# A window-attention block on one core: the projection as one fp32 product, the output product on another engine, y1 kept by row halves, new instruction orders

## The chip, the cores and the metric

One of the eight cores of a Trainium2 chip runs the whole program. The metric is the device time of one execution in microseconds, given as the median of three runs. Everything is fp32 in and out.

## The reference

The input x is (4, 96, 128, 128): four images, 96 channels. The first layer is a shifted-window transformer block, the second a divisive normalisation:

```python
y = _ln(x, norm1_w, norm1_b)                       # over the 96 channels
y = roll(y, (-4, -4)); windows of 8 x 8 = 64 tokens
qkv = y @ qkv_w.T + qkv_b                          # 6 heads of 16
attn = softmax(q * 16**-0.5 @ k.T + mask)          # mask in the last row/column of windows
out = (attn @ v) @ proj_w.T + proj_b
x = shortcut + roll_back(out)
h1 = gelu(_ln(x, norm2_w, norm2_b) @ mlp_w1.T + mlp_b1)     # 96 -> 384
x = x + (h1 @ mlp_w2.T + mlp_b2)                   # 384 -> 96
out = x * rsqrt(beta_eff + gamma_eff @ (x * x))    # over the channels
```

## The kernel before

**Tiles.** A unit is one row of 16 windows of one image (1024 tokens), 64 units in all. The work goes by halves of a unit: 8 windows, 512 tokens, 128 halves. Most tiles are 96 channels (partitions) by 512 tokens.

**Rounds.** The program is software-pipelined. `rounds` (L221) unrolls rounds H = -5 to 127, and in each round every engine runs its list `steps` in a fixed, written-out order. A stage has an offset, so in round H the stage works on half H + offset: TURN_IN 4 (transpose x, statistics), TURN_OUT 3 (transpose the normalised values back, y1), QK 1 (keys and queries), ATTEND 0 (scores, softmax, values), PROJECT -1 (division, projection, first residual), MLP -2, SETTLE -3 (second MLP product, second residual, squares), DIVIDE -4 (denominators, outputs). Each engine works its list in order and waits on semaphores; nothing is reordered at run time. The last halves are finished by `late` calls behind the rounds.

**Products.** Large products are done in parts: `in_parts` (L949) splits weight and moving operand into a rounded part (hi) and a rest (lo) of type fp32r and adds three products, hi x hi, lo(weight) x hi and hi x lo. The splits of moving operands are made by GpSimd (`split_hi` L444, `split_lo` L449: y1, attended, squares, hidden) and VectorE. The attended values are split before the projection: VectorE divides (`divide`, L821) and rounds them (`round_attended`, L831), GpSimd subtracts (`rest_of_attended`, L462), TensorE projects in three parts (`project`, L1074). Small products, the transposes and the last projection (`last_project`, L1104) are one full fp32 product each.

**Tiles of TensorE.** Scores use tiles of 32 rows x 64 columns (L1013, masks L1021), values (L986), the sums of probabilities (L1066, L1069) and attend (L1056) write 32 columns at a time, the transposes of the first two probability groups (L1033) use 64 rows, all else the whole array.

**Banks.** The products of `MM_ITEMS` (L248) take turns in two PSUM banks, in the order of that list. A product waits until the product two places ahead has been read out of its bank (`mm_wait`).

**y1.** The first layer norm's result is held per unit as [window, token]. ScalarE writes it (`y_copy`, L555) four rows of each window at a time: an even half of a unit's transposes has the upper four rows of all 16 windows, the odd half the lower four. GpSimd's `round_y1` and `rest_of_y1` take these rows through `ln_rows` (runs of 32 values), and the products read a half of 8 windows as one contiguous run of 512.

**Output.** `outputs` (L850) on VectorE multiplies x3 by the inverse denominator into `o_ext`, 4 columns to the right; GpSimd copies the columns that wrap around the edge (`wrap_out`), and the SP queue stores the unit. SP also loads x and copies the keys into block form (`copy_keys`, 6 DMAs a half).

## Time and profile before

| | |
|---|---|
| median of 3 runs | 1819.56 us (1818.24 to 1821.19) |
| profiled execution | 1816.74 us, span in the trace 1814.5 us |
| mean granted TensorE clock | 0.995 of full |
| busy DVE / ACT / POOL | 1677.5 / 1587.7 / 1553.4 us |
| DMA | 81.17 MB, mean 45 GB/s |

PE is TensorE (PEld its weight loads, which run beside the products), DVE VectorE, ACT ScalarE, POOL GpSimd, SP the queue of DMAs. The trace's products overlap in a pipeline: the duration of one is longer than the distance to the next, so the distance between two starts is what a product takes of TensorE's time. One full fp32 product is recorded as two instructions, a transpose or an fp32r product as one.

### The profile page before, as it was taken

To read this page: it belongs to the slowest core of one execution; us is meant where nothing else is said; L and a number is where in the kernel's file an instruction comes from. 1 tells how busy PE (TensorE), PEld (TensorE's weight loads), DVE (VectorE), ACT (ScalarE), POOL (GpSimd) and SP (SyncE) were. 2 spreads that over 40 slices of the span, in tenths; PEclk is the share of its full clock that TensorE was granted. 3 is DMA by queue.
4 is the path that set the end of the run, shared out by engine and by line. 5 is a ranking of instruction groups with operands and counts; after the bars stand their busy time and mean duration, and the time that the engine had idled before them with its cause. 6 is when DMAs were issued, how large, how long until landed. Compare 5 with 4: busy or idle time off the path is not lost.

```text
span 1814.5 us, 78584 instructions
## 1 busy us (share of the span) xinstructions
PE 1764.4 (97%) x31203; PEld 1344.6 (74%) x31203; DVE 1677.5 (92%) x4637; ACT 1587.7 (87%) x2700; POOL 1553.4 (86%) x1661
## 2 busy tenths in 40 slices
PE   5899999999999999999999999999999999999997
PEld 3677777777777777777777777777777777777774
DVE  5799999999999999999999999999999999999985
ACT  2799999998999899989899999899989989998895
POOL 4488999988898888998898898898888889898883
PEclk9899999999999999999999999999999999999999
DMA  2111222122122122222121221221221221221211
GB/s 57 24 42 39 49 52 42 44 52 44 43 52 45 42 52 42 45 51 43 44 50 36 52 51 37 51 51 36 52 51 35 53 50 34 54 50 33 46 34 27
DMA packets 215143, 81.17 MB, mean 45 GB/s; under 512 B 116118, under 2 KB 214780, under 8 KB 214780
## 3 DMA queue, kind: packets, MB, share of 16 engines
q1 hardware_dynamic: 214218, 76.04, 19.2%
q8 instruction: 249, 4.08, 0.9%
q14 instruction: 114, 0.93, 0.2%
q10 hardware_dynamic: 562, 0.11, 0.0%
HBM read 25.75 MB, written 25.17 MB: 28 GB/s over the span
## 4 chain that ended last, share of the span: by engine, by line
PE 95%; DVE 1%; issue 1%; ACT 1%; DMA 0%; SPq 0%; POOL 0%; POOLq 0%; DVEq 0%; ACTq 0%
PE mm_bank L952 50%; PE score_banks L1013 7%; PE turn_bank L945 7%; PE turn_bank L938 6%; PE mm_bank L986 6%; PE pv_bank L1056 5%; PE score_banks L1033 5%; PE score_banks L1042 3%; PE mm_bank L1069 3%; PE mm_bank L1066 2%; PE score_banks L1021 1%; SPq L373 0%; PE mm_bank L1116 0%; DMA k_block<-k 0%; DMA x_ext<-in_x 0%
## 5 line engine op out<-in xcount | busy, mean ns | idle before, releaser
L452 POOL TENSOR_TENSOR hidden_lo<-hidden,hidden_hi 128x512 fp32r<-128x512 f32 x378 | 480.9, 1285 | 0.0
L539 ACT ACT_TABLE_LOAD x253 | 324.6, 1283 | 4.5
L452 POOL TENSOR_TENSOR attended_lo<-attended,attended_hi 96x512 fp32r<-96x512 f32 x127 | 163.8, 1290 | 111.0 <-DVE attended_hi L834 111.0
L808 DVE TENSOR_REDUCE row_max<-score_banks 128x8 f32<-128x512 f32 x384 | 241.4, 684 | 17.8 <-PE score_banks L1021 9.9
L582 ACT ACTIVATE probs<-shifted 128x512 f32<-128x512 f32 x384 | 236.4, 629 | 20.1 <-DVE shifted L816 13.2
L816 DVE TENSOR_TENSOR shifted<-score_banks,row_max 128x512 f32<-128x512 f32 x384 | 250.8, 680 | 0.0
L615 ACT ACTIVATE hidden<-mm_bank 128x512 f32<-128x512 f32 x381 | 228.6, 600 | 20.5 <-PE mm_bank L952 2.2
L447 POOL TENSOR_SCALAR hidden_hi<-hidden 128x512 fp32r<-128x512 f32 x378 | 228.5, 615 | 4.0 <-ACT hidden L615 3.8
L765 DVE BATCH_NORM_STATS2 stats<-turn_bank 128x6 f32<-128x96 f32 x1024 | 192.8, 250 | 30.2 <-PE turn_bank L938 25.8
L594 ACT ACTIVATE probs_t<-score_banks 128x512 f32<-128x512 f32 x384 | 214.5, 594 | 5.8 <-PE score_banks L1033 4.0
L468 POOL TENSOR_TENSOR x_sq<-x 96x512 f32<-96x512 f32 x126 | 130.7, 1037 | 73.7 <-DVE x L846 66.2
L945 PE MATMUL turn_bank<-ident_sb,y_tok 128*96 128x128 f32 x1024 | 161.1, 280 | 15.3 <-DVE y_tok L783 15.2
L952 PE MATMUL mm_bank<-y_hi,w_hi 97*128 97x512 f32 x381 | 171.8, 451 | 0.2 <-ACT hidden L615 0.2
L452 POOL TENSOR_TENSOR y_lo<-y,y_hi 96x512 fp32r<-96x512 f32 x128 | 163.4, 1276 | 1.1 <-POOL y_hi L447 1.1
L452 POOL TENSOR_TENSOR x_sq_lo<-x_sq,x_sq_hi 96x512 fp32r<-96x512 f32 x126 | 163.3, 1296 | 0.7 <-POOL x_sq_hi L447 0.7
L447 POOL TENSOR_SCALAR y_hi<-y 96x512 fp32r<-96x512 f32 x128 | 142.8, 1115 | 23.5 <-ACT y L564 23.5
L1013 PEld LDWEIGHTS score_banks<-k_block,q 32*64 32x64 f32 x6144 | 116.0, 132 | 51.9 <-issue 51.9
L1013 PE MATMUL score_banks<-k_block,q 32*64 32x128 f32 x6144 | 148.9, 275 | 4.7 <-DMA k_block<-k 3.6
L774 DVE TENSOR_TENSOR turn_bank<-turn_bank,moments 128x384 f32<-128x384 f32 x256 | 145.0, 566 | 9.0
L952 PE MATMUL mm_bank<-hidden_hi,w_hi 128*96 128x512 f32 x378 | 150.7, 399 | 0.9 <-ACT k L574 0.9
L952 PE MATMUL mm_bank<-y_lo,w_hi 97*128 97x512 f32 x381 | 150.9, 396 | 0.0
L952 PE MATMUL mm_bank<-y_hi,w_lo 97*128 97x512 f32 x381 | 150.3, 394 | 0.0
(144 smaller groups left out, 4815.3 us busy)
## 6 DMA issues: line engine op xcount, KB each, us to landing
x_ext<-in_x SPq DMA_DIRECT2D x128, 192.0 KB, 3.1
k_block<-k SPq DMA_DIRECT2D x768, 32.0 KB
out<-o_ext SPq DMA_DIRECT2D x128, 192.0 KB, 2.7
w_raw<-in_w_t SPq DMA_DIRECT2D x1, 144.0 KB
w<-in_w_t SPq DMA_DIRECT2D x1, 144.0 KB
qkv_raw<-in_qkv_t ACTq DMA_DIRECT2D x1, 108.0 KB
ident_sb<-in_ident SPq DMA_DIRECT2D x1, 64.0 KB, 2.3
q_quadrants<-in_qmask SPq DMA_DIRECT2D x3, 1.0 KB
```

What stands on the lines that cost most here:

```text
L447: nc.gpsimd.tensor_scalar(hi, whole, 1.0, 1.0, ALU.mult, ALU.mult).then_inc(hi_ready, 1)
L452: nc.gpsimd.tensor_tensor(lo, whole, hi, ALU.subtract).then_inc(is_split, 1)
L539: nc.scalar.preload_act_table_set(name)
L582: nc.scalar.activation(probs[:, g, :, :, :].rearrange("t p j k -> t (p j k)"), shifted[:, g, :, :].rearrange("t i k -> t (i k)"), ACT.Exp)\
L594: nc.scalar.activation(dst, src, ACT.Copy).then_inc(probs_t_ready, 1)
L615: nc.scalar.activation(hidden_of(A)[:, n, :], up_bank(A, n), ACT.Gelu).then_inc(gelu_ready, 1)
L765: made = nc.vector.bn_stats(stats[ln][:, c, :], turn_banks[ln][:, n * DIM:(n + 1) * DIM])
L808: nc.vector.tensor_reduce(row_max[:, g, :], group_scores(g), op=ALU.max, axis=AX.X)\
L816: nc.vector.tensor_tensor(shifted[:, g, :, :], group_scores(g), row_max[:, g, :].unsqueeze(2) .broadcast_to([128, PAIRS * TILE_HEADS, TOKE ...
L945: made = nc.tensor.transpose(turn_banks[ln][0:DIM, n * 128:(n + 1) * 128], y_tok[ln][:, c, :], ident_sb[:, :])
L952: made = nc.tensor.matmul(out, w, x_part, start=first and part == 0, stop=last and part == 2)
L1013: made = nc.tensor.matmul(score_banks[64 * n:64 * n + 64, r, cols], q[rows, unit_slot(a), (w + n) * TOKENS:(w + n + 1) * TOKENS], k_block[ ...
```

## The change

- `project` multiplies the whole (unsplit) fp32 tiles `wproj` and `attended` in one full fp32 product. The hi and lo tiles, `round_attended`, `rest_of_attended`, the weight split and `last_project` go; `divide` now waits until the projection of the half before has read `attended`.
- `outputs` moves from VectorE to GpSimd, behind `wrap_x` in its list; the last four halves' outputs stay on VectorE (`last_outputs`).
- y1, y1_hi and y1_lo are kept by row halves: [half of the rows, window, 32 tokens]. What `round_y1`, `rest_of_y1` and `y_copy` handle is one contiguous run of 512; the key and query products read it as 8 windows x 2 runs of 32, the value product's weights stay runs of 32.
- New orders on TensorE, VectorE, ScalarE and GpSimd, and in `MM_ITEMS`. On TensorE the value stage goes between the sums and the attend products, the denominators ahead of both transposes back, these ahead of the queries; the first up product ahead of the residual's transposes and the last probability group.

```diff
+            ("v", ATTEND, v_ready, 1, 1),
             ("k", QK, k_ready, 1, 1),
+            ("den", DIVIDE, log_den_made, 1, 1),
             ("q", QK, q_ready, 1, 1),
-            ("den", DIVIDE, log_den_made, 1, 1),
             ("mlp2", SETTLE, x3_ready, 1, 1),
-            ("v", ATTEND, v_ready, 1, 1),
...
+        def y1_rows(tile, a):
+            return half_of(tile[:, unit_slot(a), :], a)
+
+        def y1_windows(tile, a):
+            by_window = tile[:, unit_slot(a), :].rearrange("c (h n t) -> c n h t", h=2, t=TOKENS // 2)
+            return by_window[:, half_windows(a), :, :]
...
 GpSimd
+            def outputs(A, a):
+                wait_alone(pool, inv_den_ready, A + 1)
+                if has(A - 4):
+                    wait_alone(pool, out_stored[unit_slot(a)], 32 * (A // 4))
+                nc.gpsimd.tensor_tensor(windows_of(o_ext[:, unit_slot(a), :, :], a),
+                                        in_windows(half_of(x3, a)), in_windows(inv_den[:, :]),
+                                        ALU.mult).then_inc(out_ready, 1)
...
                 run(wrap_out, DIVIDE - 1)
-                run(rest_of_attended, PROJECT)
                 run(wrap_x, TURN_IN)
+                run(outputs, DIVIDE)
+                run(round_y1, TURN_OUT)
+                run(rest_of_y1, TURN_OUT)
                 run(square, SETTLE)
                 run(round_squares, SETTLE)
-                run(round_y1, TURN_OUT)
                 run(rest_of_squares, SETTLE)
-                run(rest_of_y1, TURN_OUT)
 ScalarE
                 run(k_copy, QK)
+                run(log_denominators, DIVIDE)
+                run(softmax_exp, ATTEND, 0)
+                run(inverse_denominators, DIVIDE)
+                run(softmax_exp, ATTEND, 1)
                 run(q_copy, QK)
                 run(y_copy, MLP, 1)
-                run(softmax_exp, ATTEND, 0)
-                run(log_denominators, DIVIDE)
-                run(inverse_denominators, DIVIDE)
-                run(softmax_exp, ATTEND, 1)
+                run(y_copy, TURN_OUT, 0)
                 run(softmax_exp, ATTEND, 2)
-                run(y_copy, TURN_OUT, 0)
                 run(load_tables, MLP, "gelu_and_others")
                 run(probs_t_copy, ATTEND, 0)
+                run(gelu, MLP, 0)
                 run(probs_t_copy, ATTEND, 1)
-                run(gelu, MLP, 0)
                 run(probs_t_copy, ATTEND, 2)
 VectorE
                 run(max_scores, ATTEND, 0)
                 run(max_scores, ATTEND, 1)
-                run(max_scores, ATTEND, 2)
+                run(v_blocks, ATTEND)
+                run(normalise, TURN_OUT, 0)
                 run(normalise, MLP, 1)
                 run(shift_scores, ATTEND, 0)
+                run(shift_scores, ATTEND, 1)
                 run(divide, PROJECT)
-                run(normalise, TURN_OUT, 0)
-                run(round_attended, PROJECT)
-                run(shift_scores, ATTEND, 1)
+                run(max_scores, ATTEND, 2)
                 run(shift_scores, ATTEND, 2)
                 run(second_residual, SETTLE)
                 run(split_y2, MLP)
-                run(v_blocks, ATTEND)
                 run(first_residual, PROJECT)
-                run(outputs, DIVIDE)
 TensorE
-                pe.wait_ge(attended_split, A + 1)
+                pe.wait_ge(attended_ready, A + 1)
                 mm_wait("proj", A)
-                in_parts(mm_bank("proj", A)[0:DIM, :], wproj_hi[:, :], wproj_lo[:, :],
-                         attended_hi[:, :], attended_lo[:, :]).then_inc(proj_made, 1)
+                nc.tensor.matmul(mm_bank("proj", A)[0:DIM, :], wproj[:, :], attended[:, :],
+                                 start=True, stop=True).then_inc(proj_made, 1)
...
                 run(scores, ATTEND)
                 run(sum_probs, ATTEND - 1)
+                run(project_v, ATTEND)
                 run(times_v, ATTEND - 1)
                 run(project_k, QK)
+                run(denominators, DIVIDE)
+                run(turn_out, TURN_OUT, 0)
+                run(turn_out, MLP, 1)
                 run(project_q, QK)
-                run(turn_out, MLP, 1)
-                run(denominators, DIVIDE)
                 for n in range(HID_CHUNKS):
                     run(mlp_down, SETTLE, n)
-                run(project_v, ATTEND)
-                run(turn_out, TURN_OUT, 0)
                 run(project, PROJECT)
                 run(turn_two_groups, ATTEND)
                 run(turn_in, TURN_IN, 0)
...
+                run(mlp_up, MLP, 0)
+                run(turn_in, PROJECT, 1)
                 run(turn_last_group, ATTEND)
-                run(mlp_up, MLP, 0)
                 run(mlp_up, MLP, 1)
-                run(turn_in, PROJECT, 1)
                 run(mlp_up, MLP, 2)
```

## Rows read from the trace of the kernel before

**Rows 1.** The page's busy times, shares of the span and numbers of instructions.
```profile
PE 1764.4 (97%) x31203; PEld 1344.6 (74%) x31203; DVE 1677.5 (92%) x4637; ACT 1587.7 (87%) x2700; POOL 1553.4 (86%) x1661
```
**Rows 2.** The chain that ended last, shares by engine.
```profile
PE 95%; DVE 1%; issue 1%; ACT 1%; DMA 0%; SPq 0%; POOL 0%; POOLq 0%; DVEq 0%; ACTq 0%
```
**Rows 3.** TensorE's waits from 100 to 1750 us: total, times, longest.
```profile
PE pv_bank L1056 <- issue: 5.5, 9, 0.8
...
```
**Rows 4.** Busy time (and instructions) by engine in a window, then clock and DMA.
```profile
900.00:927.00 27.00, 27.00 (x484) 20.71 (x483) 25.11 (x71) 24.50 (x43) 23.98 (x26) 1.00 0.21 47
```
**Rows 5.** Timeline of TensorE's products, one round: start, duration, instruction.
```profile
907.98 1.11 PE L1013 MATMUL score_banks<-k_block,q 32*64 32x128 f32 x48
...
911.73 0.40 PE L952 MATMUL mm_bank<-y_lo,wq_hi 97*96 97x512 f32 x1
911.96 0.60 PE L945 MATMUL turn_bank<-ident_sb,y_tok 128*96 128x128 f32 x4
912.32 0.47 PE L952 MATMUL mm_bank<-x_sq_hi,wgdn_hi 97*96 97x512 f32 x1
...
914.96 0.40 PE L952 MATMUL mm_bank<-hidden_lo,w_hi 128*96 128x512 f32 x1
915.28 0.89 PE L986 MATMUL mm_bank<-wv,y 97*32 97x48 f32 x64
916.10 0.64 PE L945 MATMUL turn_bank<-ident_sb,y_tok 128*96 128x128 f32 x4
916.50 0.47 PE L952 MATMUL mm_bank<-attended_hi,wproj_hi 97*96 97x512 f32 x1
...
917.37 0.71 PE L1033 MATMUL score_banks<-ident_sb,probs 64*128 64x64 f32 x16
...
921.39 1.12 PE L1013 MATMUL score_banks<-k_block,q 32*64 32x128 f32 x48
```
**Rows 6.** Timeline of weight loads of the last full fp32 products.
```profile
1800.54 0.16 PEld L1116 LDWEIGHTS mm_bank<-hidden,w 128*96 128x96 f32 x1 [0.27 <-issue]
...
1801.82 0.16 PEld L1116 LDWEIGHTS mm_bank<-hidden,w 128*96 128x96 f32 x1 [0.27 <-issue]
```
**Rows 7.** Timeline, products at the same place.
```profile
1799.87 0.39 PE L952 MATMUL score_banks<-y_lo,w_hi 97*128 97x512 f32 x1
1800.10 2.74 PE L1116 MATMUL mm_bank<-hidden,w 128*96 128x512 f32 x6
```
**Rows 8.** Timeline of weight loads in the sampled round, behind idle time.
```profile
909.02 0.12 PEld L1066 LDWEIGHTS mm_bank<-probs_t,ones_pair_sb 128*32 128x32 f32 x3 [0.17 <-issue]
...
915.28 0.75 PEld L986 LDWEIGHTS mm_bank<-wv,y 97*32 97x32 f32 x64 [0.40 <-issue]
```
**Rows 9.** GpSimd's groups; the first row gives least, middle and greatest ns.
```profile
L447 POOL TENSOR_SCALAR y_hi<-y x128: 612/1145/1156, 14.1 to 1738.3; 96x512 fp32r<-96x512 f32 x128
...
L452 POOL TENSOR_TENSOR attended_lo<-attended,attended_hi 96x512 fp32r<-96x512 f32 x127 | 163.8, 1290 | 111.0 <-DVE attended_hi L834 111.0
...
L468 POOL TENSOR_TENSOR x_sq<-x 96x512 f32<-96x512 f32 x126 | 130.7, 1037 | 73.7 <-DVE x L846 66.2 <-issue 7.3
...
L441 POOL COPY x_ext<-x_ext 96x32 f32<-96x32 f32 x64 | 13.3, 208 | 2.0 <-DMA x_ext<-in_x 1.7 <-POOL x_sq L433 0.3
```
**Rows 10.** VectorE's only squaring of x3 into x3_sq, as a group.
```profile
L756 DVE TENSOR_TENSOR x_sq<-x 96x512 f32<-96x512 f32 x1 | 0.7, 690 | 0.3 <-DVE x L846 0.3
```
**Rows 11.** Timelines of VectorE and GpSimd at 904.7 us.
```profile
904.72 0.68 DVE L853 TENSOR_TENSOR o_ext<-x,inv_den 96x512 f32<-96x512 f32 x1
...
904.73 1.14 POOL L447 TENSOR_SCALAR y_hi<-y 96x512 fp32r<-96x512 f32 x1
```
**Rows 12.** Timeline of ScalarE in the sampled round.
```profile
913.65 0.59 ACT L620 ACTIVATE log_den<-mm_bank 96x512 f32<-96x512 f32 x1
...
916.78 0.59 ACT L564 ACTIVATE y<-turn_bank 96x512 f32<-96x512 f32 x1 [0.48 <-PE turn_bank L945]
...
920.29 0.59 ACT L594 ACTIVATE probs_t<-score_banks 128x512 f32<-128x512 f32 x1
```

More of the change, by code:

```diff
@@ L57 @@
 MLP_CONSTS = 9
-MLP_WEIGHTS = 4
+MLP_WEIGHTS = 3
 TURN_IN, TURN_OUT, QK, ATTEND, PROJECT, MLP, SETTLE, DIVIDE = 4, 3, 1, 0, -1, -2, -3, -4
@@ L95, in window_block @@
         w2 = sb("w2", [128, HID_CHUNKS, DIM])
-        wq_hi, wq_lo, wk_hi, wk_lo, wproj_hi, wproj_lo, wgdn_hi, wgdn_lo = (
+        wq_hi, wq_lo, wk_hi, wk_lo, wgdn_hi, wgdn_lo = (
             sb(f"{name}_{part}", [DIM + 1, DIM], f32r)
-            for name in ("wq", "wk", "wproj", "wgdn") for part in ("hi", "lo"))
+            for name in ("wq", "wk", "wgdn") for part in ("hi", "lo"))
         w1_hi, w1_lo = (sb(f"w1_{part}", [DIM + 1, HIDDEN], f32r) for part in ("hi", "lo"))
@@ L427, in set_rows @@
             def set_rows():
-                for hi, lo in ((y2_hi, y2_lo), (attended_hi, attended_lo), (x3_sq_hi, x3_sq_lo)):
+                for hi, lo in ((y2_hi, y2_lo), (x3_sq_hi, x3_sq_lo)):
                     nc.gpsimd.memset(hi[DIM:DIM + 1, :].bitcast(f32), 1.0).then_inc(rows_set, 1)
@@ L454, in round_y1 @@
             def round_y1(A, a):
-                split_hi(ln_rows(y1_hi[0:DIM, unit_slot(a), :], a), ln_rows(y1[0:DIM, unit_slot(a), :], a),
+                split_hi(y1_rows(y1_hi, a)[0:DIM], y1_rows(y1, a)[0:DIM],
                          y_ready[0], y1_hi_ready, A + 1)
             def rest_of_y1(A, a):
-                hi, lo, whole = (ln_rows(tile[0:DIM, unit_slot(a), :], a) for tile in (y1_hi, y1_lo, y1))
+                hi, lo, whole = (y1_rows(tile, a)[0:DIM] for tile in (y1_hi, y1_lo, y1))
                 split_lo(hi, lo, whole, y1_hi_ready, y1_split, A + 1)
-            def rest_of_attended(A, a):
-                split_lo(attended_hi[0:DIM, :], attended_lo[0:DIM, :], attended[0:DIM, :],
-                         attended_hi_ready, attended_split, A + 1)
             def square(A, a):
@@ L823, in divide @@
                 dve.wait_ge(pv_made, A + 1)
+                wait(dve, proj_made, A)
                 for m in range(HEAD_PAIRS):
@@ L889, in _ @@
             late(statistics, FINAL, 1)
-            late(outputs, FINAL - 3)
+            last_outputs(FINAL - 3)
             late(normalise, FINAL, 1)
@@ L894, in _ @@
             late(last_squares, FINAL - 1)
-            late(outputs, FINAL - 2)
+            last_outputs(FINAL - 2)
             late(second_residual, FINAL)
             late(last_squares, FINAL)
-            late(outputs, FINAL - 1)
-            late(outputs, FINAL)
+            last_outputs(FINAL - 1)
+            last_outputs(FINAL)
         @block.tensor
@@ L962, in project_k @@
                 mm_wait("k", A)
-                rows = slice(0, DIM + 1)
                 in_parts(mm_bank("k", A)[0:DIM, :], wk_hi[:, :], wk_lo[:, :],
-                         half_of(y1_hi[rows, unit_slot(a), :], a), half_of(y1_lo[rows, unit_slot(a), :], a))\
+                         y1_windows(y1_hi, a), y1_windows(y1_lo, a))\
                     .then_inc(k_made, 1)
@@ L984, in project_v @@
                         for part in range(2):
-                            first, to = n * TOKENS + 32 * part, 64 * e + 32 * part
+                            to = 64 * e + 32 * part
                             made = nc.tensor.matmul(mm_bank("v", A)[to:to + 32, n * width:(n + 1) * width],
-                                                    half_of(y1[:, unit_slot(a), :], a)
-                                                    [:, first:first + 32],
+                                                    y1_windows(y1, a)[:, n, part, :],
                                                     wv[:, e, :, :], start=True, stop=True)
@@ L1102, in mlp_down @@
                     made.then_inc(mlp2_made, 1)
-            def last_project():
-                pe.wait_ge(attended_ready, FINAL + 1)
-                mm_wait("proj", FINAL)
-                nc.tensor.matmul(mm_bank("proj", FINAL)[0:DIM, :], wproj[:, :], attended[:, :],
-                                 start=True, stop=True).then_inc(proj_made, 1)
             def last_mlp_down(A):
@@ L1163, in _ @@
             late(denominators, FINAL - 3)
-            last_project()
+            late(project, FINAL)
             for n in range(HID_CHUNKS):
```

28 lines of the change are left out of this document (9 added, 19 removed).

## The prediction

> **What bounds the kernel now.** I read the shares of busy time first, then the chain, then who waited, then one round in order of time. TensorE is busy 1764.4 of 1814.5 us [rows 1], and the chain of work that ended last lies on it for 95% [rows 2]. From 100 to 1750 us its waits on all other engines and DMAs come to nothing: the list holds only stops "issue", 5.5 us in 9 pieces [rows 3]. In a sample of two rounds it is busy 27.00 of 27.00 us at full clock, VectorE 25.11, ScalarE 24.50, GpSimd 23.98 [rows 4]. So a round is as long as TensorE's own queue: from one score stage to the next 921.39 - 907.98 = 13.41 us [rows 5] (odd halves add mask products, which the change leaves alone). What the others do counts only if one of them, or a wait, becomes longer than TensorE's queue. The sum is therefore one of TensorE start-to-start intervals, not of busy times, which overlap.
>
> **Part 1, projection in full fp32.** Before: three fp32r products, from the first start at 916.50 to the start of the next stage at 917.37, 0.87 us [rows 5]. That holds 3 x 0.23 (an fp32r product that another follows without a switch takes 911.96 - 911.73 = 0.23), 0.09 for leaving the whole array for the small tiles of the probability transposes (the same step is 915.28 - 914.96 = 0.32 ahead of the value stage), and the remaining 0.09 for entering fp32r from another kind [rows 5]. After: one fp32 product, which the trace records as two instructions. At the end of the kernel such instructions load weights every (1801.82 - 1800.54)/3 = 0.427 us [rows 6], so the product takes 0.85 us, not less than the three that it replaces (0.70). Going over from fp32r to it costs nothing (1800.10 - 1799.87 = 0.23 [rows 7]), so the entry goes. The exit to small tiles no row shows behind an fp32 product: it is 0 at best and 0.09 as behind fp32r. I take 0.09, the nearest row. New stage 0.94 us: +0.07 a half; with a free exit -0.02.
>
> **Part 2, TensorE's order.** The value stage (32-column tiles) moves from between two whole-array stages to between the probability sums and the attend products, which use 32-column tiles too. Gone are the exit ahead of it, 0.09, and what follows it: the stage spans 916.10 - 915.28 = 0.82 us, its weight loads 0.75 [rows 5, 8], so 0.07. The layer-norm transposes behind it took 0.40 (916.50 - 916.10); behind an fp32r product the same four take 912.32 - 911.96 = 0.36 [rows 5], and that is where they now stand: 0.04. The number of entries into fp32r outside the projection stays four (key/denominator, query/down, first up, the last two ups; before key/query, denominator/down, first two ups, last up), and a whole-array transpose behind fp32r enters free as before. Together -0.20. If the three neighbours don't share a tile setting, each border costs what the one from scores to sums does: weight loads stand 0.17 us [rows 8]. Bounds -0.20 to -0.20 + 2 x 0.17 = +0.14; I take -0.20, since sums and attend products, both 128 x 32, follow each other with no such gap.
>
> **Part 3, y1 by row halves.** The key and query products now read runs of 32 values, two runs a window, where they read 512 in one piece; each of the 6 reads is the same 512 columns. No row has TensorE reading so. Nearest row: GpSimd's rounding of y1 reads and writes runs of 32 in all its 128 executions and took 612 ns at its least, 1145 in the middle [rows 9], so the runs are not what costs there. Upper end: each takes the slower 0.427 of the fp32 instruction, + 6 x 0.20 = 1.2 us a half. I take 0. [...]
>
> **Part 4, GpSimd and VectorE.** VectorE loses the rounding of the attended values and the output product (0.68): 12.56 - 0.68 = under 11.9 us a half [rows 4, 11]. GpSimd loses the attended rest (1290) and gains the output product. Its y1 rounding mostly took 1145 ns but can take 612 [rows 9]; in the sample it starts at 904.73, VectorE's output product, the one VectorE instruction here with both inputs in SBUF, at 904.72 [rows 11]. I read the surplus 0.53 as two engines getting in each other's way, and it goes in either reading (stride or collision). The output product on GpSimd, X: at least the square's 1.04, near the 1.29 of the subtraction that goes [rows 9]; at most, with runs of 8, the rate of the wrap copies, 208 ns for 32 values, x 16 = 3.3 us [rows 9]. I take 1.2. GpSimd then is busy 11.99 - 1.29 - 0.53 + 1.2 = 11.4 us a half, with three waits on its own last result of 0.2 each 12.0; room until 13.28, that is until X = 2.5.
>
> [...] The trace has the same squaring on both, 1037 against 690 ns [rows 9, 10], a ratio of 1.5.
>
> **Part 5, the waits of the new order.** Lay the new TensorE round out by the intervals above: scores 0, sums 1.05, values 1.72, attend 2.47, keys 3.26, denominator 4.03, two transposes 4.7, queries 5.4, down 6.2, projection 8.3, first group transposes 9.2, up 10.2, last group 11.6, up 12.4, next scores 13.28. The key product comes 0.75 later, and with it the copy to k_block; all transfers had a whole half of slack (no such wait in [rows 3]). The projection no longer waits for rounding and rest: division is reached on VectorE after about 5.7 and ends at 7.2, 1 us early. Tightest is ScalarE: from the denominator's logarithm to the start of the last probability copy it took 920.29 - 913.65 = 6.64 [rows 12], 0.48 of it idle; one exponential, the query copy and one turned copy join this stretch, 3 x 0.5, the second gelu's place is behind it. So it starts at 4.95 + 7.6 = 12.5, ends 13.1 and releases the scores due at 13.28: 0.2 to spare. ScalarE's total of 12.25 a half is unchanged. GpSimd's in-order queue puts output, y1 and squares behind hidden's split; output can start near 6.9 (inverse denominator), the rest follows by 12.2 + X, the split for the next half then ends at 4.7 + X of the next round, ahead of the down products at 6.2 as long as X is under 1.5, and in any case ahead of the output that it queues before. The down products take three splits in turn, so a late last split is met only from X of about 2.2. Cost taken: 0.
>
> **The sum.** +0.07 - 0.09 - 0.07 - 0.04 = -0.13 us a half, round 13.28. The projection is replaced 127 times: -16.5 us. The first rounds and the end, where nearly all of TensorE's 50.1 us of idle time lies [rows 1, 3], I take as unchanged, +-3. The profiled execution ran 1816.74 us around its span of 1814.5, 2.8 below the median of 1819.56; median after 1803.1 us.
>
> **Rivals.** (a) More gain: the exit behind the fp32 product is free, -0.22 a half, -28 us, 1791.6. For it: an fp32 instruction's weight loads leave 0.27 us open [rows 6]; against it: every switch to small tiles seen here has its gap. (b) A wash: the value stage keeps its drains between its new neighbours for a part, or ScalarE's 0.2 us is overdrawn by as much as TensorE gains (0.13): 1819. (c) Slower: tiles of 97 rows and of 128 rows don't mix, and both borders of the value stage cost 0.17. It decides at once, in every half: -0.13 + 0.34 = +0.21, +27 us, 1846. For it: the 0.17 between two tiled stages [rows 8]; against it: sums to attend is seamless. (d) Slower: GpSimd becomes the bound from X = 2.5; at 3.3 the round is 10.77 + 3.3 = 14.1, +0.7, +86 us, 1905. Against it: stride cost GpSimd nothing in the y1 rounding. (e) Slower: strided reads slow the key and query products; it decides from 0.13/6 = 0.022 us each, at the upper end +1.2 - 0.13, +136 us, 1955. (f) The change does not shorten the GpSimd rounding: changes no time, since it is covered.
>
> **How the numbers follow.** Forecast 0.60, (a) 0.10, (b) 0.12, (c) 0.10, (d) 0.04, (e) 0.04. This kernel's measurement tells a change from none at about 0.2%, 3.6 us. Faster: forecast and (a), 0.70; same 0.12; slower 0.18. The forecast's own range is 1796 to 1811 (the exit and the ends); for 8 in 10 it reaches to (a) and over (b) into part of (c): 1790 to 1826.
>
> **What would show it.** Right: projection two instructions, 0.94 to the next start; no gap in weight loads ahead of the value stage; rounds of 13.28; y1 rounding 615; key and query products still 0.23 apart; TensorE still without waits. Wrong: waits of the scores for the probability copies, of the down products for hidden's split, output on GpSimd over 2 us, or gaps around the value stage.

## The result, and the profile after: slower by 1.9%

The changed kernel took 1857.01 us (median of 4 runs, 1854.67 to 1859.94) against 1820.38 for the kernel before on the same chip: a ratio of 1.019, with a 95% interval of 1.0168 to 1.0212. Forecast were 1803.1 us and a range up to 1826. The prediction was wrong in sign, and none of its rivals names what happened.

The page of the changed kernel: span and busy times, the fetches of instructions, and the chain that ended last.

```profile
span 1857.9 us, 78073 instructions
PE 1779.8 (96%) x31076; PEld 1348.0 (73%) x31076; DVE 1595.3 (86%) x4384; ACT 1552.2 (84%) x2704; POOL 1490.7 (80%) x1656
...
q8 instruction: 248, 4.06, 0.9%
...
PE 94%; issue 2%; DVE 1%; ACT 1%; DMA 1%; SPq 1%; POOL 0%; POOLq 0%; DVEq 0%
```

VectorE, ScalarE and GpSimd all do less than in [rows 1], and TensorE's list is still the path, so the time is lost in TensorE's own queue. Its waits from 100 to 1750 us (total, times, longest):

```profile
PE pv_bank L1054 <- issue: 22.9, 41, 1.2
PE mm_bank L985 <- issue: 8.8, 10, 1.4
PE mm_bank L952 <- issue: 0.6, 1, 0.6
```

In [rows 3] the first line read 5.5 us in 9 pieces. The same view of the kernel before has one line more, so 6.4 us in 10 pieces altogether:

```profile
PE mm_bank L952 <- issue: 0.9, 1, 0.9
```

"issue" means that no semaphore and no transfer of data is seen to release the engine. Three stretches of TensorE's timeline: a round without a stop (869.68), one with a stop (911.42, shown from its sums on), and the products behind a third stop.

```profile
869.68 1.12 PE L1011 MATMUL score_banks<-k_block,q 32*64 32x128 f32 x48
870.73 0.52 PE L1064 MATMUL mm_bank<-probs_t,ones_pair_sb 128*32 128x384 f32 x3
...
871.40 0.87 PE L985 MATMUL mm_bank<-wv,y 97*32 97x48 f32 x63
...
872.09 0.88 PE L1054 MATMUL pv_bank<-probs_t,v_block 128*32 128x64 f32 x47
872.89 0.48 PE L952 MATMUL mm_bank<-y_hi,wk_hi 97*96 97x512 f32 x1
873.21 0.40 PE L952 MATMUL mm_bank<-y_hi,wk_lo 97*96 97x512 f32 x1
873.44 0.40 PE L952 MATMUL mm_bank<-y_lo,wk_hi 97*96 97x512 f32 x1
873.68 0.39 PE L952 MATMUL mm_bank<-x_sq_hi,wgdn_hi 97*96 97x512 f32 x1
...
877.82 0.40 PE L952 MATMUL mm_bank<-hidden_lo,w_hi 128*96 128x512 f32 x1
878.05 1.02 PE L1078 MATMUL mm_bank<-attended,wproj 97*96 97x512 f32 x2
879.00 0.71 PE L1031 MATMUL score_banks<-ident_sb,probs 64*128 64x64 f32 x16
...
914.02 0.89 PE L985 MATMUL mm_bank<-wv,y 97*32 97x48 f32 x64
915.44 0.88 PE L1054 MATMUL pv_bank<-probs_t,v_block 128*32 128x64 f32 x48 [0.52 <-issue]
...
929.70 0.75 PE L1054 MATMUL pv_bank<-probs_t,v_block 128*32 128x64 f32 x35 [0.52 <-issue]
```

Attend products start 0.68 us behind the values at 871.40, but 1.42 behind them at 914.02 (the list counts 0.52 of these 0.74 us, since a product's recorded duration runs on past its share). At 929.70 the stop falls inside the stage: 13 of its 48 products are done, 35 are left, and no wait stands there in the kernel.

Measuring all 127 distances from one score stage to the next splits the change of span, 1857.9 - 1814.5 = 43.4 us:

| | before | after | difference |
|---|---|---|---|
| undisturbed round, even / odd half | 13.40 / 13.63 | 13.35 / 13.58 | -0.05 each, -6.6 in all with those at the end of an image |
| excess over that, rounds that have one | 10.5 us in 12 | 46.6 us in 57 | +36.1 (ends of an image +1.7) |
| first five rounds | 69.6 | 71.6 | +2.0 |
| from the last score stage to the end | 46.5 | 55.7 | +9.2 |

The remaining 1 us lies ahead of the first round and in the last two.

The end has a cause of its own. ScalarE's timeline behind the last round:

```profile
1812.56 1.28 ACT L544 ACT_TABLE_LOAD   x1
...
1816.98 1.28 ACT L554 ACT_TABLE_LOAD   x1
1818.27 0.30 ACT L554 ACTIVATE log_var<-moments,eps_col 128x4 f32<-128x4 f32 x1
1818.59 1.28 ACT L557 ACT_TABLE_LOAD   x1
1819.88 0.21 ACT L557 ACTIVATE rstd<-log_var 128x4 f32<-128x4 f32 x1
1820.10 1.28 ACT L602 ACT_TABLE_LOAD   x1
1821.40 0.49 ACT L602 ACTIVATE log_sum<-mm_bank 128x384 f32<-128x384 f32 x1
1821.90 1.28 ACT L609 ACT_TABLE_LOAD   x1
```

A table load stands ahead of every logarithm and every exponential, eight in all. The diff moves `run(load_tables, MLP - 1, "natural_log_exp_and_others")` from the end of ScalarE's list to its start. Within the rounds that is the same sequence; behind the last round the list no longer loads the set ahead of these functions, and each gets a load of its own, eight of 1.28 us. In e9, with one load by hand there, none of the eight is in the trace.

### The profile page after: what moved, and what is told of

It is laid out like the page before. It is cut to its first block, busy times and chain, and to the rows that moved or that the text cites. A ratio compares the mean times of both kernels' runs of the same rounds, so it can differ in the third digit from the quotient of the medians.

```text
span 1857.9 us, 78073 instructions
## 1 busy us (share of the span) xinstructions
PE 1779.8 (96%) x31076; PEld 1348.0 (73%) x31076; DVE 1595.3 (86%) x4384; ACT 1552.2 (84%) x2704; POOL 1490.7 (80%) x1656
## 3 DMA queue, kind: packets, MB, share of 16 engines
q8 instruction: 248, 4.06, 0.9%
## 4 chain that ended last, share of the span: by engine, by line
PE 94%; issue 2%; DVE 1%; ACT 1%; DMA 1%; SPq 1%; POOL 0%; POOLq 0%; DVEq 0%
PE mm_bank L952 44%; PE score_banks L1011 8%; PE turn_bank L945 6%; PE mm_bank L1078 6%; PE turn_bank L938 6%; PE pv_bank L1054 6%; PE mm_bank L985 5%; PE score_banks L1031 4%; PE mm_bank L1067 3%; PE score_banks L1040 3%; PE mm_bank L1064 2%; PE score_banks L1019 1%; SPq L373 0%; DMA k_block<-k 0%; PE mm_bank L1107 0%
## 5 line engine op out<-in xcount | busy, mean ns | idle before, releaser
L452 POOL TENSOR_TENSOR hidden_lo<-hidden,hidden_hi 128x512 fp32r<-128x512 f32 x378 | 480.4, 1285 | 0.0
L811 DVE TENSOR_REDUCE row_max<-score_banks 128x8 f32<-128x512 f32 x384 | 251.7, 683 | 67.5 <-PE score_banks L1019 47.4
L493 POOL TENSOR_TENSOR o_ext<-x,inv_den 96x512 f32<-96x512 f32 x124 | 160.4, 1293 | 129.5 <-ACT inv_den L631 129.5
L578 ACT ACTIVATE k<-mm_bank 96x512 f32<-96x512 f32 x128 | 76.2, 595 | 168.7 <-PE mm_bank L952 168.7
L452 POOL TENSOR_TENSOR y_lo<-y,y_hi 96x512 fp32r<-96x512 f32 x128 | 163.8, 1279 | 23.5 <-POOL y_hi L447 13.6
L452 POOL TENSOR_TENSOR x_sq_lo<-x_sq,x_sq_hi 96x512 fp32r<-96x512 f32 x126 | 161.7, 1284 | 23.1 <-POOL x_sq_hi L447 23.1
L447 POOL TENSOR_SCALAR y_hi<-y 96x512 fp32r<-96x512 f32 x128 | 79.0, 617 | 124.1 <-ACT y L568 124.1
L1011 PEld LDWEIGHTS score_banks<-k_block,q 32*64 32x64 f32 x6144 | 120.3, 133 | 50.3 <-issue 50.3
L802 DVE TENSOR_TENSOR v_block<-mm_bank,ones_pair_sb 128x768 f32<-128x768 f32 x128 | 122.6, 958 | 39.2 <-PE mm_bank L985 39.1
L945 PE MATMUL turn_bank<-ident_sb,y_tok 128*96 128x128 f32 x1024 | 136.1, 275 | 15.8 <-DVE y_tok L786 15.8
```

Of the source, the lines that this page charges most:

```text
L447: nc.gpsimd.tensor_scalar(hi, whole, 1.0, 1.0, ALU.mult, ALU.mult).then_inc(hi_ready, 1)
L452: nc.gpsimd.tensor_tensor(lo, whole, hi, ALU.subtract).then_inc(is_split, 1)
L811: nc.vector.tensor_reduce(row_max[:, g, :], group_scores(g), op=ALU.max, axis=AX.X)\
L945: made = nc.tensor.transpose(turn_banks[ln][0:DIM, n * 128:(n + 1) * 128], y_tok[ln][:, c, :], ident_sb[:, :])
L1011: made = nc.tensor.matmul(score_banks[64 * n:64 * n + 64, r, cols], q[rows, unit_slot(a), (w + n) * TOKENS:(w + n + 1) * TOKENS], k_block[ ...
```

## The experiments

"Round" is the undisturbed one, even / odd; "stops" is TensorE's idle time on "issue" from 100 to 1750 us; "end" runs from the last score stage. In e2, e4 and e12 nearly every round waits or stops, and e11 is paced by a wait; for these four the median of all later rounds stands. Each ratio is to runs of the kernel before on the same chip; their median was 1819.2 to 1820.7 us, for e12 1829.8. Of the times forecast below, only those of e6 and e10 came, and in e11 the rival's; what tells the theories apart are the stops, the rounds and the ends.

| run | median us | ratio to before (95%) | round | stops | end |
|---|---|---|---|---|---|
| before, after | 1820.4, 1857.0 | 1, 1.019 | 13.40/13.63, 13.35/13.58 | 6.4, 32.3 | 46.5, 55.7 |
| e1 values early | 1874.7 | 1.029 (1.0269-1.031) | 13.73/13.89 | 40.1 | 46.9 |
| e2 values back | 1872.5 | 1.0286 (1.0271-1.0302) | 14.12/14.07 | 0.3 | 55.0 |
| e3 blocks off | 1872.5 | 1.029 (1.0267-1.0312) | 13.81/14.00 | 2.2 | 54.9 |
| e4 blocks on | 1963.9 | 1.0784 (1.076-1.0807) | 14.71/14.69 | 49.7 | 54.3 |
| e5 values mid | 1842.5 | 1.0129 (1.0108-1.015) | 13.66/13.87 | 0.2 | 55.4 |
| e6 squares first | 1831.3 | 1.007 (1.0048-1.0093) | 13.60/13.82 | 0 | 54.4 |
| e7 fp32 projection | 1846.2 | 1.0147 (1.0126-1.0167) | 13.57/13.79 | 13.9 | 49.4 |
| e8 wide values | 1852.1 | 1.0178 (1.0154-1.0201) | 13.66/13.89 | 7.0 | 49.4 |
| e9 table load | 1852.0 | 1.0178 (1.016-1.0196) | 13.36/13.57 | 37.2 | 46.7 |
| e10 e6 + table load | 1824.1 | 1.0021 (1.0008-1.0034) | 13.60/13.82 | 0.3 | 46.4 |
| e11 orders alone | 1839.0 | 1.0098 (1.008-1.0117) | 13.76/13.76 | 0.9 | 52.2 |
| e12 split projection | 1958.6 | 1.0724 (1.0691-1.0758) | 14.87/14.90 | 0.7 | 50.2 |

**e1 and e2: does the place of the values make the stops?** e1 is the kernel before with one move; e2 is the changed kernel with that move undone (and with it the first transposes back and the copy of y1).

```diff
                 run(sum_probs, ATTEND - 1)
+                run(project_v, ATTEND)          # e1; e2 takes it out here
                 run(times_v, ATTEND - 1)
...
                     run(mlp_down, SETTLE, n)
-                run(project_v, ATTEND)          # e1; e2 puts it in here
```

> The kernel before, with one edit: the value stage (and its bank place and its copy on VectorE) stands between the probability sums and the attend products. Theory F (instruction feed): TensorE now meets scores, sums, values and attend in one run of 172 short load-and-multiply pairs instead of 108, and its stream of instructions can't be supplied that fast whenever the end of a block of 256 instructions falls late in the run. Then undisturbed rounds get shorter by up to 0.2 us, but about half of the rounds show 0.3 to 1.2 us of idle time with no releaser inside the values or attend products: about 1835 to 1850 us, slower than before. Rival R (the fp32 projection, or the other moved stages, make the waits): this kernel keeps the old projection and all other orders, so it loses nothing and is at most 1820, near 1797 by the predicted gain of 0.20 a half.

> The changed kernel, with the value stage and the transposes behind it back between the down products and the projection (bank place, VectorE's copy and ScalarE's y1 copy moved with them). Theory F: the bursts of long rounds go, idle time without a releaser falls from some 32 us to under 8, and what is left is the dearer projection (+0.08 a half, 10 us) over the kernel before: 1822 to 1835. Rival R: the bursts stay, 1850 or more.

Stops follow the place of the values: 6.4 to 40.1 us by moving them alone, 32.3 to 0.3 by moving them back. Neither run became faster, because each order is tied to the rest. In e1 attend and division come 0.7 us later, and the rest of attended meets the projection late (`POOL attended_lo L452`: 7.9 us of waits of the products in 48 pieces, 26.6 of the weight loads in 74), so that even its rounds without a stop take 13.73 / 13.89. In e2 GpSimd is last. Its timeline in e2:

```profile
910.63 0.62 POOL L447 TENSOR_SCALAR y_hi<-y 96x512 fp32r<-96x512 f32 x1 [2.10 <-ACT y L568]
...
914.71 1.27 POOL L452 TENSOR_TENSOR x_sq_lo<-x_sq,x_sq_hi 96x512 fp32r<-96x512 f32 x1 [0.18 <-POOL x_sq_hi L447]
915.95 1.20 POOL L447 TENSOR_SCALAR hidden_hi<-hidden 128x512 fp32r<-128x512 f32 x2
```

It waits 2.10 us for y1, with the squares and the next split of hidden queued behind, and the down products wait for hidden's rest (11.4 us in 53 pieces).

**e3 and e4: what do the stops hang on?** TensorE's list holds 63,693 instructions in the trace of the changed kernel: two for each of the 31,076 products (weight load, product) and 1541 waits and the like. The page shows 248 packets of 4.06 MB / 248 = 16 KB on q8, "instruction"; that is 4.06 MB / 63,693 = 64 bytes an instruction and 63,693 / 248 = 257 instructions a packet, so I take a packet as a block of 256, and the places of the stops bear it out. Counted through the trace, all 52 stops from 100 to 1750 us come at instruction 192 or 193 modulo 256, and the 10 stops of the kernel before at 193 or 194: always at the same place, an end of a block. (The count starts at the first instruction traced, so only that the place stays the same means something.) A round has 486 (even) or 498 (odd) instructions, so block ends drift by 26 or 14 a round through the stages; the stops come in bursts with 44, 31, 24, 11, 4 attend products left. e3 adds waits for a semaphore that has long been reached, until each round has 512 instructions, so that ends of blocks always fall in the same two places: by that count early in the values and in the down products (1.94 and 7.90 us behind the start of the scores in round 50). e4 is e3 with 110 such waits more in the first rounds alone, which moves both ends into the run of short products, one into the scores and one late into the attend products (0.50 and 3.26 us).

```diff
+            FILL = [54, 52, 14, 26, ...]        # e4: [54, 54, 54, 54, 54, 26, ...]
...
+                    for _ in range(min(2, fill[0])):
+                        wait_alone(pe, ident_loaded, 16)
+                        fill[0] -= 1
```

> The changed kernel with waits on a long satisfied semaphore put among the fp32r products (14 or 26 a round, 2788 in all), so that every ordinary round has exactly 512 TensorE instructions; the ends of the blocks of 256 then fall at instructions 144 and 400 of each round, early in the values and in the down products. Nothing else changes. Theory F: hardly any idle time without a releaser, all rounds near 13.35 and 13.58 us as in the undisturbed stretches, plus what the waits themselves take (up to 0.1 a round if they hide behind 0.23 us products): 1808 to 1825. Rival R, and any cause that doesn't go by the count of instructions: the same bursts, 1857 or a little more.

> The same with 110 waits more in the first rounds only, so that the block ends fall at instructions 34 and 290, late in the attend products, in every round. Theory F: a stop in nearly every round, 0.5 us or more each, some 120 stops: 1875 to 1930. Rival R: the same time as with the ends off the dense run, within 3 us.

TensorE's waits in the same stretch, of e3:

```profile
PE pv_bank L1060 <- issue: 1.6, 3, 0.7
PE mm_bank L991 <- issue: 0.6, 3, 0.2
```

and of e4:

```profile
PE pv_bank L1060 <- issue: 43.5, 98, 0.8
PE mm_bank L958 <- issue: 4.6, 4, 1.7
```

The same work, the same data, in every later round the same instructions: 91.5 us between them, at the attend products 98 stops against 3. Of the 98.0 us between the two spans, 75.5 lie between the start of the sums and that of the keys (rounds 8 to 124), where these stops are. Where the block ends fall decides.

e3 itself isn't faster than the changed kernel, as the waits added cost more than they save. Even rounds are 0.46 us longer with 26 of them, odd ones 0.42 with 14. In even rounds all of it lies in the keys and denominators, right behind the short products, which have 12 of the 26: from the scores to the transposes back 5.16 us for 4.70. From there to the projection, with the other 14, both kernels take 3.67.

The trace also shows the fetch. The DMA view of the changed kernel from 912.80 to 913.30 us (busy share in 40 slices, packets, queue):

```profile
DMA  0000000000000000000000009000000000000000
...
DMA packets 1, 0.02 MB, mean 33 GB/s; under 512 B 0, under 2 KB 0, under 8 KB 0
...
q8 instruction: 1, 0.02, 12.0%
```

The one packet lies in slice 25, at 912.80 + 24 x 0.0125 = 913.10, and the stop ends 2.34 us behind it, at 915.44. So it is at seven stops from 785 to 945 us: packets at 785.30, 800.25, 843.05, 898.65, 913.10, 927.35 and 941.55, ends of the stops at 788.06, 802.62, 845.56, 900.92, 915.44, 929.70 and 944.02, 2.27 to 2.76 us later. Behind six of them the next packet comes 1.1 to 3.1 us after the stop. Over the whole trace no block's first instruction runs less than 2.16 us behind the start of its packet: all 52 stops end 2.2 to 2.9 us behind it, while at the block ends without a stop the packet is mostly long there (179 of the 231 ends from 100 to 1750 us, median 8.0 us). A block of short pairs goes by in about that time, 2.4 us by my estimate: scores, sums, values and attend are now 172 pairs in a row, 344 instructions in 3.2 us (869.68 to 872.89), where before the longest run was 108 pairs in 2.5. The new run is longer than a block: where one end falls among the attend products, the end before it lies 256 instructions earlier, in the scores or just ahead of them, and the whole block between the two is short pairs.

**e5 and e6: the changed kernel without the run of 172.** e5 puts the values behind the denominators; e6 is e2 with GpSimd's squares ahead of y1.

```diff
-                run(project_v, ATTEND)          # e5
                 run(times_v, ATTEND - 1)
                 run(project_k, QK)
                 run(denominators, DIVIDE)
+                run(project_v, ATTEND)
...
-                run(round_y1, TURN_OUT)         # e6, on GpSimd, over e2
-                run(rest_of_y1, TURN_OUT)
                 run(square, SETTLE)
                 run(round_squares, SETTLE)
                 run(rest_of_squares, SETTLE)
+                run(round_y1, TURN_OUT)
+                run(rest_of_y1, TURN_OUT)
```

> The changed kernel, with the value stage behind the denominators instead of ahead of the attend products (bank place moved with it, VectorE's copy behind the second shift). GpSimd's and ScalarE's orders are untouched, so the late y1 that held back the version with the values behind the down products can't arise. Theory F: the dense run is 108 pairs again and six fp32r products part it from the 64 of the values; idle time without a releaser falls to 10 us or less, the round is 13.35 + 0.1 to 0.2 for the value stage's own drains: 1815 to 1830 us. Rival R2 (the changed order as a whole, not the length of the run, makes the stops): idle time without a releaser stays above 25 us and the time near 1857.

> The version with the values back behind the down products, with GpSimd's squares and their split ahead of y1's rounding and rest. There the round was 14.08 us without stops; I read that as a ring: values, transposes, y1 copy, y1 rounding and rest, squares, hidden's split, down products, values. Theory (ring): squares no longer wait for y1, the ring opens, rounds fall to about 13.5 and the time to 1815 to 1835. If the ring isn't it, the time stays at 1872.

e5 has one stop of 0.2 us, e6 none, and both beat the changed kernel, though their undisturbed rounds are 0.24 to 0.31 us longer. In e5, where only the values moved, that is the price of the values' own borders, and it bears out the gain forecast for moving them; the stops took it back. e6 against e2, 41 us by the order of five GpSimd instructions, shows that e2 had been held up by the queue on GpSimd and not by TensorE's order.

**e7: the fp32 projection alone**, in the kernel before. **e8: half as many value products** of 64 columns each, in the kernel before.

```diff
-                in_parts(mm_bank("proj", A)[0:DIM, :], wproj_hi[:, :], wproj_lo[:, :],   # e7
-                         attended_hi[:, :], attended_lo[:, :]).then_inc(proj_made, 1)
+                nc.tensor.matmul(mm_bank("proj", A)[0:DIM, :], wproj[:, :], attended[:, :],
+                                 start=True, stop=True).then_inc(proj_made, 1)
...
-                        for part in range(2):                                   # e8
-                            first, to = n * TOKENS + 32 * part, 64 * e + 32 * part
-                            made = nc.tensor.matmul(mm_bank("v", A)[to:to + 32, n * width:(n + 1) * width],
-                                                    half_of(y1[:, unit_slot(a), :], a)
-                                                    [:, first:first + 32],
+                        made = nc.tensor.matmul(mm_bank("v", A)[64 * e:64 * e + 64, n * width:(n + 1) * width],
+                                                half_of(y1[:, unit_slot(a), :], a)
+                                                [:, n * TOKENS:(n + 1) * TOKENS],
```

> The kernel before with the projection as one full fp32 product; the rounding on VectorE and the rest on GpSimd go, all orders stay. From the start-to-start intervals 0.95 in place of 0.87 us a half: +10 us if TensorE bounds it as before, 1827 to 1833. If the projection were the cause of the change's loss (rival R): 1850 or more. If the missing split opens something: at or under 1820.

> The kernel before with the 32 value products of a half (64 weight loads and 64 passes, tiles of 32 columns) made as 16 with tiles of 64 columns: 64 instructions a round less, the same sums. Theory F: 422 or so instructions a round instead of 486, fewer block ends and a lighter run: the 10 stops of before go or nearly (-8 us), the value stage itself takes 32 pairs at the 22 ns of the score stage, 0.70 instead of 0.75 (-6 us): 1800 to 1812. If instructions don't matter: 1814 to 1820.

TensorE's timeline in e7:

```profile
912.40 0.64 PE L944 MATMUL turn_bank<-ident_sb,y_tok 128*96 128x128 f32 x4
912.88 1.02 PE L1079 MATMUL mm_bank<-attended,wproj 97*96 97x512 f32 x2
913.84 0.71 PE L1032 MATMUL score_banks<-ident_sb,probs 64*128 64x64 f32 x16
```

The projection takes 0.96 us there, and the transposes ahead of it 0.48 where [rows 5] have 0.40. Half of e7's 0.165 us a round is the border in front. The time, 1846.2 us, missed its range of 1827 to 1833: besides 21 us in the rounds (127 x 0.165) the stops rose from 6.4 to 13.9 us (21 of them) and the end from 46.5 to 49.4, and for neither was a cause tested. e8's expectation failed, in the stops too (7.0 us in 13). TensorE's timeline in e8:

```profile
906.52 1.14 PE L984 MATMUL mm_bank<-wv,y 97*64 97x48 f32 x32
907.59 0.64 PE L945 MATMUL turn_bank<-ident_sb,y_tok 128*96 128x128 f32 x4
```

The 32 wide products take 1.07 us, the 64 narrow ones 0.82 [rows 5]; fewer instructions were not less work.

**e9 and e10: the table load**, in the changed kernel and in e6.

```diff
             rounds(steps)
+            late(load_tables, FINAL, "natural_log_exp_and_others")
```

> The changed kernel with one ScalarE instruction more: behind the last round the table set of natural logarithm and exponential is loaded once, by hand. Theory of the end: in the changed kernel the round's own load stands at the start of ScalarE's list, so behind the last round the gelu set stays loaded and eight loads of 1.28 us stand one ahead of each logarithm and exponential of the last layer norms and softmax, 9.2 us of end in all (55.7 against 46.5 us from the last score stage on). Then one load does, the end comes back to 46.5 to 48 us, the rounds stay as they are, and the time is 1857 - 8 to 9 = 1848 to 1849. Rival: the end is long because TensorE's clock falls there or because its work is late for another reason, and the loads stand beside it; then the loads go and the end stays over 53 us, 1855 to 1857.

> The version that keeps the fp32 projection and has the values back between the down projection and the projection, with GpSimd's squares ahead of y1 (1831.3, end of 54.4 us, almost no stops of TensorE), and the one table load behind the rounds. If the end and the rounds are separate costs, the same 8 us come off here: 1822 to 1824, end 46 to 48 us. If what remains over the kernel before is in the end alone, it would be at 1819 or less; by the rounds (13.60/13.82 against 13.40/13.63, 0.2 x 126 = 25 us, less 9 us of stops and about 8 us of the first rounds) I expect it 2 to 5 us above the kernel before. Rival: GpSimd is what ends these rounds, and the time follows it; then still 1822, but waits of TensorE for GpSimd of over 5 us stand in the rounds.

ScalarE behind the last round in e9:

```profile
1815.15 1.28 ACT L544 ACT_TABLE_LOAD   x1
1816.45 0.30 ACT L554 ACTIVATE log_var<-moments,eps_col 128x4 f32<-128x4 f32 x1
1816.78 0.20 ACT L557 ACTIVATE rstd<-log_var 128x4 f32<-128x4 f32 x1
1816.89 0.47 ACT L602 ACTIVATE log_sum<-mm_bank 128x384 f32<-128x384 f32 x1
```

The end came back to 46.7 and 46.4 us, as the first theory said. TensorE's granted clock from 1815 to 1830 us was 0.67 of full in the changed kernel, where TensorE waited behind ScalarE's loads (2.96 us up to 1820.73, 2.18 up to 1825.28), and 0.93 in e9, so the loads cost twice, in time and in clock (with a granted clock of 0.50, as from 1821 to 1823 us of the changed kernel, an fp32r product of 512 columns is recorded with 0.63 us, at 1822.04, instead of 0.39). e10's median fell by 7.2 us, close to the forecast; e9's by 5.0 instead of 8 to 9. The span of e9's profiled run fell by 10.8 us, 9.0 of it in the end (its first rounds took 6.6 less and its stops 4.9 more), so the mechanism is shown and the missing 3 to 4 us of the median are not assigned.

**e11 and e12: can both be had?** e11 gives the kernel before the orders of e10 and nothing else; e12 gives e10 the split projection back.

```diff
+                run(denominators, DIVIDE)       # e11, on TensorE; the other lists to match
+                run(turn_out, MLP, 1)
                 run(project_q, QK)
-                run(turn_out, MLP, 1)
-                run(denominators, DIVIDE)
...
                 run(outputs, DIVIDE)            # e12, on GpSimd
+                run(rest_of_attended, PROJECT)
...
                 run(divide, PROJECT)            # e12, on VectorE
+                run(round_attended, PROJECT)
```

> The kernel before with its projection split as it was, its outputs on VectorE and its y1 whole, and only orders changed: TensorE gets k, denominators, MLP's way back, q, down, values, the first way back, projection, two groups, and each way up behind its own way in; ScalarE's, VectorE's and the small matmul's lists follow it. Theory of the stops: the dense run of short pairs is again broken between attend and values, so there are at most a few stops (excess under 12 us), and the rounds keep the split projection (0.87 and its cheap transposes, 0.165 a half less than in fp32): 13.44/13.66 or less, first rounds 62 to 66, 1800 to 1812 in all, so faster than the kernel before. Rival: what made the orders affordable was GpSimd taking the outputs; with them on VectorE (outputs 1.36, squares 0.69 a round, VectorE busy 13.3 of 13.5 us) VectorE ends the round, TensorE waits for it more than 10 us, and the time is 1820 to 1840.

> The version of the run before last but one (values between the down projection and the projection, squares first, outputs on GpSimd, y1 by row halves, one table load behind the rounds: 1824.1) with the projection split in three again as in the kernel before: VectorE casts the attended values (0.42), GpSimd makes the rest (1.29) behind the outputs. Theory, that the fp32 projection is what makes that version's rounds long: its price alone was 0.165 a half, so the rounds go from 13.60/13.82 to 13.44/13.66, the time to 1824 less 21 = 1803 to 1807, faster than the kernel before, whose stops (10.5 us) and slow first rounds (69.6 against 61.5) it leaves behind. GpSimd would be at 11.8 + 1.3 = 13.1 us of 13.55. Rival: GpSimd's queue ends the round. The outputs end at 7.4 us behind the start of the scores and the rest of attended at 8.7, which is 0.1 to 0.2 late for the projection at 8.55, and each wait ahead of the squares then falls on the next round: rounds of 13.7 or more, 1825 to 1845, with waits of TensorE for GpSimd's attended_lo in over half of the rounds.

In e11 the rival's time came, 1839.0 us, its sign only in part: the list of TensorE's products has 0.9 us of waits, not over 10. VectorE's waits in e11 from 100 to 1750 us are short:

```profile
DVE row_max L808 <- PE score_banks L1021: 14.4, 57, 1.1
```

Even and odd rounds are alike, 13.76 us, as they are when the pace is VectorE's (busy 1695.1 us, 1677.5 in [rows 1]) and not TensorE's with its mask products in every other half. The place is the projection: it starts 8.87 us behind the scores in even rounds and 8.88 in odd ones, 8.52 and 8.74 in the kernel before, while GpSimd waits 92.4 us for VectorE's rounding of the attended values in 119 pieces. So these orders are paid for by what left VectorE. e12 missed by far, in the rival's direction and well beyond it. GpSimd in e12:

```profile
907.75 1.30 POOL L501 TENSOR_TENSOR o_ext<-x,inv_den 96x512 f32<-96x512 f32 x1 [0.30 <-ACT inv_den L640]
909.51 1.27 POOL L456 TENSOR_TENSOR attended_lo<-attended,attended_hi 96x512 fp32r<-96x512 f32 x1 [0.46 <-DVE attended_hi L855]
```

and VectorE:

```profile
907.76 1.57 DVE L855 CAST attended_hi<-attended 96x512 fp32r<-96x512 f32 x1
```

The cast, 0.41 us in the trace of before, starts together with GpSimd's output product and ends only behind it: 1.57 us here, 1.36 on average over the 111 from 100 to 1750 us. It is the collision of [rows 11] (there GpSimd's rounding took 1.14 us, at its least 0.61 [rows 9]) with the parts exchanged, and this time it falls on the path: VectorE is late, then the rest of attended (TensorE's weight loads wait 131 us for it in 111 pieces), then the residual (TensorE's products wait 102.6 us for it in 94).

The collision is not the whole of it. In 17 of the 111 rounds the cast takes 0.42 us (in most of these the output product starts beside it and takes 1.58 instead of 1.30), and such a round lasts 14.11 us, mostly, where the others last 14.73 to 14.9. So the collision costs some 0.8 us a round. But 14.11 is still above e10's 13.60 / 13.82, with the projection at 9.21 us behind the scores for 8.85 there in odd rounds: that much the longer way through cast and rest costs without it, which is the rival's reading.

## Why the prediction was wrong, step by step

- **The step that failed is the first: "a round is as long as TensorE's own queue", added up from starts.** [Rows 3] showed 5.5 us of "issue" in 9 stops at the attend products, and the prediction read that as nothing. It said that the list holds only these; the whole list has 6.4 us in 10. The sum had no term for bringing TensorE's instructions, and the change lengthens just that run, from 108 short pairs to 172. This cost +36 us; that it is the supply of instructions is shown by e3 against e4, e1, e2 and the packets ahead of the stops. The sign of it was in the trace before: the stops stand in the middle of a stage, where the kernel has no wait, and q8's 249 packets stood on the page.
- **"The first rounds and the end, [...], I take as unchanged, +-3"** failed as well: +9.2 us at the end, from one line of the diff that changes no round. e9 and e10 show it. The steps were read round by round; what the last round leaves behind was not.
- **Part 1, +0.07, right:** 879.00 - 878.05 = 0.95 us (forecast 0.94), entry from fp32r free (878.05 - 877.82 = 0.23). Where transposes stand ahead instead it is twice as dear (e7, 0.165 a round).
- **Part 2, -0.20, right in size:** values 0.68 for 0.82, down products 2.09 for 2.19, attend 0.02 more, so -0.22. The 0.04 at the transposes did not come: the eight in a row take 0.79, two fours took 0.76. Taken apart, the borders are worth 0.31 a round (e5).
- **Part 3, 0, right:** keys start at 873.21, 873.44 and 873.68, 0.23 apart, with y1 read in runs of 32.
- **Part 4, no cost, right:** GpSimd's output product took 1.29 us (taken: 1.2), y1's rounding 0.62. That is 1.9 times VectorE's 0.68 [rows 11]. The ratio of 1.5 from the squares, 1.02 us by it, was too low, but 1.29 is well inside the 2.5 that GpSimd had room for. e12 adds what no ratio of two durations prices: there the product on GpSimd holds up a cast on VectorE, 1.57 us for 0.42.
- **Part 5, 0, half right:** no engine came late. But the new neighbours cost TensorE 0.10 us a round: queries +0.09, keys +0.02, denominators -0.07, transposes in both directions and ups +0.06. By stages the undisturbed even round is -0.22 + 0.08 + 0.10 = -0.04 (13.36 from 869.68, against 13.40) where the sum had -0.13: some 10 us of the 54 missed.
- **Rivals:** (c) gave 1846, near the truth, by a mechanism that did not occur: values between sums and attend took 0.68 us, without either border. That it came near is luck. No version tried beats the kernel before; e10 comes nearest, at 1.0021.

**Open.** The length of the run isn't all: with the same 108 pairs, the kernels with the old order of the up products have 10 to 21 stops (before, e7, e8), those with the new order 0 to 3 (e2, e5, e6, e10, e11, e12). The order of the up products, just ahead of the scores, was not varied alone. What makes the chip ask for the next block at the moment it does: the packets after a stop come at no fixed distance. The first five rounds vary between 61.5 and 73.9 us without a cause that was tested, and the end takes 49.4 to 52.2 in e7, e8, e11 and e12 without repeated table loads.

## What to carry to other kernels

A queue that never waits for another engine can still run dry, as TensorE's did here for 32.3 us in 52 stops: count the instructions in each dense run of small products, and take an "issue" stop inside a stage, however small its sum, as a sign of how near the supply is; part such runs by long products rather than lining them up (e5, with six fp32r products between them, has 0.2 us of stops). Gains from joining like stages and losses from a long run of them come from one and the same edit (here 0.31 us a round gained, as e5 shows, and 36.1 us in all lost to stops), so price both. When a stateful instruction (a table load) moves within a loop, follow the list past the last round too (9.2 us here).

## What the hardware showed unexpectedly

- The packet with a block of 256 TensorE instructions starts 2.2 to 2.9 us before the block is first used at a stop (52 stops of the changed kernel), about as long as 256 instructions of short pairs take (2.4 us at the dense run's 344 in 3.2 us). At the other 179 block ends from 100 to 1750 us the change of block costs no stop, the packet starting 8.0 us ahead in the median; what the stops can cost where both ends of a round fall in the dense run is the 91.5 us between e3 and e4.
- Waits on a semaphore already reached cost TensorE 0.46 us for 12 of them right behind the run of short products, and nothing for 14 among later products of the same kind (e3, even rounds).
- A VectorE cast within SBUF that starts together with GpSimd's two-input product mostly lasts until that ends, 1.57 us for 0.41: in 94 of the 111 rounds of e12 from 100 to 1750 us it ends 0.28 to 0.29 us behind the product (909.33 and 909.05 in the timelines above). In the other 17 the cast takes 0.42 to 0.43, and in most of them it is the product that is longer, 1.58 for 1.30. Why one of the two is drawn out was not shown.
- 32 fp32 products of 64 columns take longer than 64 of 32 columns: 1.07 us (e8) against 0.82 [rows 5].
